# SyncE reads the first role straight from the input; the first chunks of W_down and x change queues

## The chip, the cores and the metric

One core of one Trainium2 chip. The metric is device time in microseconds of one launch. The core has TensorE (PE, with PEld for its weight loads), VectorE (DVE), ScalarE (ACT), GpSimd (POOL) and SyncE (SP), and 16 DMA engines that all queues share. A name with q behind it (SPq, ACTq) is the engine's sequencer, where register loads and the issuing of DMAs show.

## What is computed

For each of 8 batches an adapter is chosen by a role number (0 to 2). With `x` of 512 rows by 1024:

```python
h = einsum('bsh,bhk->bsk', x, W_down[role]) + b_down[role]   # K = 512
h = gelu(h)
u = einsum('bsk,bkh->bsh', h, W_up[role]) + b_up[role]
y = x + u
out = layernorm(y) * gamma[role] + beta[role]
```

All is f32. The eight role numbers are the input `roles`.

## The kernel before

Every operand of a matmul is held as two parts, hi (the value rounded to fp32r by ScalarE) and lo (the rest, subtracted by VectorE), and each product is made of three passes, hi by hi, hi by lo, lo by hi. A batch has a down stage (96 matmuls of 128x512, line 254) and an up stage (96 matmuls, line 261), so TensorE runs 16 stages of 96 matmuls.

`x` (transposed, `xT`) and `W_down` come in four parts (`NLOAD`) of 128x1024, each made of two chunks of 512 columns. ScalarE casts a part (`x_hi`, L331; `wd_hi`, L335), VectorE subtracts (`x_lo`, L498; `wd_lo`, L503), TensorE multiplies. Part 0 of batch 0 alone is loaded, and cast, as two separate chunks: x at L219 and L220, W_down at L223 and L224, cast at L445, L447, L449 and L451. ScalarE casts these in a fixed order: x chunk 0, x chunk 1, W_down chunk 0, W_down chunk 1. TensorE starts the first down stage when x chunk 0 and W_down chunk 0 are cast (L283, L284); its second group of 24 matmuls needs part 1 of both.

W_down is picked by the role of the batch, so its address needs the role in a register of SyncE. ScalarE's first instruction is the DMA of the eight roles into the tile `roles_sb` (L440), the second that of `b_down` (L441); SyncE issues both x chunks, waits for `roles_landed` (L221), reads the role with `load_role` (a register load from the tile, a range check by register operations and an assertion, L140), and then issues W_down's chunks and, alternating, the other parts of x and W_down and the four parts of W_up (L161, L164, L174), all on its own queue. Then come, in a hand-written order with semaphore waits, the loads for batch 1, `b_up`, the rows of x, gamma and beta.

While data is on the way TensorE runs `WARM_UP` = 12 matmuls of bf16 zeros (L320, L321), from the moment VectorE has cleared their tile (L641). ScalarE's wait for GpSimd's constants and a first Gelu that loads the activation table (L443) stand between its DMA issues and its first cast.

Behind the up stage, per 128-row tile, VectorE adds bias rows (`bias_tile`, L520) and the residual (`sum_tile`, L525), ScalarE makes mean and variance (L369 to L372), GpSimd the inverse deviation (L467, L469), VectorE centres and finishes (L542, L556), and a DMA stores. VectorE's work is in one hand-written order, in which the `h_lo` parts (L513) that the next up stage waits for (L315) stand behind bias tiles and the splits for the next batch.

Of the kernel before, what the change touches and what calls it, by code (L numbers as in the profile page):

```python
# [16 lines left out]
def bass_role_adapter_layernorm(  # L17
# [11 lines left out]
):  # L29
    B, S, H = x.shape  # L30
    R, _, K = W_down.shape
    HC = H // P
    KC = K // P
    NT = S // P
    NLOAD = 4
    CPL = HC // NLOAD
    BANK = 512
    HALVES = H // BANK
    WARM_UP = 12
    assert KC == NLOAD and S == BANK and K == BANK and HALVES == 2 and NT == 4 and CPL == 2  # L40

    with ExitStack() as ctx:  # L42
        def sb(name, shape, dt):
            return ctx.enter_context(nc.sbuf_tensor(name, shape, dt))

        def sem(name):
            return ctx.enter_context(nc.semaphore(name))


        x_stage = sb("x_stage", [P, NLOAD, CPL * S], F32)  # L50
        wd_stage = sb("wd_stage", [P, NLOAD, CPL * K], F32)
# [39 lines left out]
        roles_landed = sem("roles_landed")  # L91
# [6 lines left out]
        first_x_landed = sem("first_x_landed")  # L98
        first_wd_landed = sem("first_wd_landed")
# [36 lines left out]
        scaled = sem("scaled")  # L136
        normed = sem("normed")

        def load_role(eng, batch):
            return eng.value_load(roles_sb[0:1, bass.ds(batch, 1)], min_val=0, max_val=R - 1)  # L140

# [2 lines left out]
        def is_first(batch):  # L144
            return isinstance(batch, int) and batch == 0

        def is_last(batch):
            return isinstance(batch, int) and batch == B - 1
# [2 lines left out]

        @block.sync
        def _(sp):
            def x_src(batch):
                return xT[batch].rearrange("(p n c) s -> p n (c s)", n=NLOAD, c=CPL)

            def wd_src(role):
                return W_down[role].rearrange("(p n c) k -> p n (c k)", n=NLOAD, c=CPL)

            def load_x_part(batch, i):  # L160
                sp.dma_start(x_stage[:, i, :], x_src(batch)[:, i, :]).then_inc(x_landed[i], 16)  # L161

            def load_wd_part(role, i):
                sp.dma_start(wd_stage[:, i, :], wd_src(role)[:, i, :]).then_inc(wd_landed[i], 16)  # L164

            def load_ahead(batch, role, i):

                sp.wait_ge(x_split, NLOAD * (batch - 1) + i + 1)
                load_x_part(batch, i)
                sp.wait_ge(wd_split, NLOAD * (batch - 1) + i + 1)  # L170
                load_wd_part(role, i)

            def load_wu_part(role, i):
                sp.dma_start(wu_stage[:, i, :], W_up[role, i * P:(i + 1) * P, :]).then_inc(wu_landed[i], 16)  # L174

            def load_rows(b, t):
                if not is_first(b):
                    sp.wait_ge(stored[t], 16 * b)
                sp.dma_start(rows[:, t, :], x[b, t * P:(t + 1) * P, :]).then_inc(rows_landed[t], 16)

            def load_role_row(row, param, role, landed):
                sp.dma_start(row[:, :], param[bass.ds(role, 1), :].partition_broadcast(P)).then_inc(landed, 16)

            def store_last(t):
                b = B - 1
                sp.wait_ge(normed, NT * b + t + 1)
                sp.dma_start(out[b, t * P:(t + 1) * P, :], rows[:, t, :]).then_inc(stored[t], 16)

            def steps(b):
                first, last = is_first(b), is_last(b)  # L190
                role = load_role(sp, b)
                load_rows(b, 0)
                load_rows(b, 1)
                if not first:
                    load_rows(b, 2)
                    sp.wait_ge(normed, NT * b)
                load_role_row(gamma_row, gamma, role, gamma_landed)
                load_role_row(beta_row, beta, role, beta_landed)
                if first:
                    load_rows(b, 2)  # L200
                load_rows(b, 3)
                if last:
                    return
                next_role = load_role(sp, b + 1)
                if first:
                    for i in range(1, NLOAD):
                        load_ahead(1, next_role, i)
                for i in range(KC):
                    sp.wait_ge(wu_split, KC * b + i + 1)
                    load_wu_part(next_role, i)  # L210
                sp.wait_ge(biased, NT * (b + 1))
                load_role_row(b_up_row, b_up, next_role, b_up_landed)
                if isinstance(b, int) and b + 2 == B:
                    return
                role_after = load_role(sp, b + 2)
                for i in range(NLOAD):
                    load_ahead(b + 2, role_after, i)

            sp.dma_start(x_stage[:, 0, 0:S], x_src(0)[:, 0, 0:S]).then_inc(first_x_landed, 16)  # L219
            sp.dma_start(x_stage[:, 0, S:CPL * S], x_src(0)[:, 0, S:CPL * S]).then_inc(x_landed[0], 16)  # L220
            sp.wait_ge(roles_landed, 16)  # L221
            first_role = load_role(sp, 0)
            sp.dma_start(wd_stage[:, 0, 0:K], wd_src(first_role)[:, 0, 0:K]).then_inc(first_wd_landed, 16)  # L223
            sp.dma_start(wd_stage[:, 0, K:CPL * K], wd_src(first_role)[:, 0, K:CPL * K]).then_inc(wd_landed[0], 16)  # L224
            for i in range(1, NLOAD):
                load_x_part(0, i)
                load_wd_part(first_role, i)
            for i in range(KC):
                load_wu_part(first_role, i)
            load_ahead(1, load_role(sp, 1), 0)  # L230
            load_role_row(b_up_row, b_up, first_role, b_up_landed)
            steps(0)
            with sp.Fori(1, B - 2) as b:
                steps(b)
            steps(B - 2)
            steps(B - 1)
            for t in range(NT - 1):
                store_last(t)
            for i in range(HALVES):
                sp.wait_ge(normed, NT * B + i)  # L240
                half = slice(i * BANK, (i + 1) * BANK)
                sp.dma_start(out[B - 1, (NT - 1) * P:NT * P, half], rows[:, NT - 1, half]).then_inc(last_stored, 16)
            for t in range(NT - 1):
                sp.wait_ge(stored[t], 16 * B)
            sp.wait_ge(stored[NT - 1], 16 * (B - 1))
            sp.wait_ge(last_stored, 16 * HALVES)

        @block.tensor
        def _(pe):
# [69 lines left out]
            pe.wait_ge(zeros_ready, 1)  # L319
            for _ in range(WARM_UP):  # L320
                pe.matmul(up_ps[:, 0, 0:BANK], squares[:, 0:P], squares[:, 0:BANK], start=True, stop=True)  # L321
# [6 lines left out]
        def _(act):  # L328
# [24 lines left out]
            def store(b, t):  # L353
                act.wait_ge(normed, NT * b + t + 1)
                act.dma_start(out[b, t * P:(t + 1) * P, :], rows[:, t, :]).then_inc(stored[t], 16)
# [54 lines left out]
            def steps(b):  # L410
# [26 lines left out]
                if not last:  # L437
                    store(b, 1)

            act.dma_start(roles_sb[:, :], roles).then_inc(roles_landed, 16)  # L440
            act.dma_start(b_down_all[:, :], b_down_cols).then_inc(b_down_landed, 16)  # L441
            act.wait_ge(constants_ready, 2)
# [236 lines left out]
```

## Time and profile before

| what | us |
|---|---|
| three timed runs | 366.93, 367.15, 368.8 |
| median of them | 367.15 |
| the profiled execution | 365.34 |
| span of its instructions | 363.5 |
| TensorE busy | 353.5 (97% of the span) |
| VectorE, ScalarE, GpSimd busy | 287.7, 185.9, 40.4 |
| the chain that ended last, by engine | PE 96%, DMA 1% |

The span runs from the first to the last instruction; the execution's own time is 1.84 us longer (365.34 to 363.5). The chain that ended last names at each step what released the next; share of it on an engine is time that only this engine's work could shorten.

### The profile page before, as it was taken

To read this page: it belongs to the slowest core of one execution; us is meant where nothing else is said; L and a number is where in the kernel's file an instruction comes from. 1 tells how busy PE (TensorE), PEld (TensorE's weight loads), DVE (VectorE), ACT (ScalarE), POOL (GpSimd) and SP (SyncE) were. 2 spreads that over 40 slices of the span, in tenths; PEclk is the share of its full clock that TensorE was granted. 3 is DMA by queue.
4 is the path that set the end of the run, shared out by engine and by line. 5 is a ranking of instruction groups with operands and counts; after the bars stand their busy time and mean duration, and the time that the engine had idled before them with its cause. 6 is when DMAs were issued, how large, how long until landed. Compare 5 with 4: busy or idle time off the path is not lost.

```text
span 363.5 us, 4942 instructions
## 1 busy us (share of the span) xinstructions
PE 353.5 (97%) x1548; PEld 289.8 (80%) x1548; DVE 287.7 (79%) x293; ACT 185.9 (51%) x297; POOL 40.4 (11%) x71
## 2 busy tenths in 40 slices
PE   7999999999999999999999999999999999999991
PEld 3888888888888888888888888888888888888880
DVE  2897989897896889968798687977789777864474
ACT  4893556671646536563385733656255561714132
POOL 0000221002200212002110021100310012200011
PEclk9999999999999999999999999999999999999998
DMA  7999999979868977869787896778977812580023
GB/s 210 408 404 412 409 404 401 330 272 377 304 231 288 308 293 261 272 252 331 248 264 247 284 374 222 224 273 276 392 267 231 289 58 101 200 278 0 0 115 116
DMA packets 27083, 96.59 MB, mean 266 GB/s; under 512 B 3138, under 2 KB 3138, under 8 KB 27074
## 3 DMA queue, kind: packets, MB, share of 16 engines
q1 hardware_dynamic: 22896, 81.80, 63.2%
q10 hardware_dynamic: 4178, 14.69, 10.5%
q8 instruction: 4, 0.07, 0.1%
q14 instruction: 5, 0.04, 0.1%
HBM read 79.70 MB, written 16.78 MB: 265 GB/s over the span
## 4 chain that ended last, share of the span: by engine, by line
PE 96%; DMA 1%; ACT 0%; DVE 0%; POOL 0%; issue 0%; SPq 0%; DVEq 0%; POOLq 0%; ACTq 0%
PE down_ps L254 48%; PE up_ps L261 48%; DMA wd_stage<-W_down 1%; DMA roles_sb<-roles 0%; DVE rows L556 0%; POOL half_var L475 0%; DVE rows L533 0%; SPq L140 0%; DVEq L42 0%; ACT wd_hi L449 0%; ACT squares L389 0%; POOLq L42 0%; ACT neg_mean_scaled L382 0%; POOL var_eps L478 0%; ACT neg_mean L384 0%
## 5 line engine op out<-in xcount | busy, mean ns | idle before, releaser
L254 PE MATMUL down_ps<-x_hi,wd_hi 128*128 128x512 f32 x256 | 81.5, 389 | 1.0 <-ACT wd_hi L449 1.0
L254 PE MATMUL down_ps<-x_lo,wd_hi 128*128 128x512 f32 x256 | 81.4, 389 | 0.0
L254 PE MATMUL down_ps<-x_hi,wd_lo 128*128 128x512 f32 x256 | 81.4, 389 | 0.0
L261 PE MATMUL up_ps<-wu_hi,h_hi 128*128 128x512 f32 x256 | 79.6, 389 | 0.0
L261 PE MATMUL up_ps<-wu_lo,h_hi 128*128 128x512 f32 x256 | 79.5, 389 | 0.0
L261 PE MATMUL up_ps<-wu_hi,h_lo 128*128 128x512 f32 x256 | 79.4, 389 | 0.0
L254 PEld LDWEIGHTS down_ps<-x_hi,wd_hi 128*128 128x128 f32 x256 | 48.0, 188 | 11.5 <-issue 1.5
L261 PEld LDWEIGHTS up_ps<-wu_hi,h_hi 128*128 128x128 f32 x256 | 48.0, 188 | 10.2 <-issue 0.3
L261 PEld LDWEIGHTS up_ps<-wu_lo,h_hi 128*128 128x128 f32 x256 | 48.0, 188 | 10.0
L254 PEld LDWEIGHTS down_ps<-x_hi,wd_lo 128*128 128x128 f32 x256 | 48.0, 188 | 10.0
L254 PEld LDWEIGHTS down_ps<-x_lo,wd_hi 128*128 128x128 f32 x256 | 48.0, 188 | 10.0
L261 PEld LDWEIGHTS up_ps<-wu_hi,h_lo 128*128 128x128 f32 x256 | 48.0, 188 | 9.9
L556 DVE SCALAR_TENSOR_TENSOR rows<-h_full,rstd,beta_row 128x1024 f32<-128x1024 f32 (+1 forms) x33 | 41.2, 1250 | 18.3 <-POOL rstd L469 17.0
L369 ACT ACTIVATE neg_mean_scaled<-row_sum 128x1 f32<-128x1 f32 x31 | 6.3, 203 | 85.7 <-DVE rows L525 85.7
L467 POOL TENSOR_TENSOR var_eps<-var,eps 128x1 f32<-128x1 f32 x31 | 15.4, 498 | 312.1 <-ACT squares L372 312.1
L542 DVE SCALAR_TENSOR_TENSOR h_full<-rows,neg_mean,gamma_row 128x1024 f32<-128x1024 f32 (+1 forms) x33 | 41.2, 1250 | 6.1 <-ACT neg_mean L370 5.5
L498 DVE TENSOR_TENSOR x_lo<-x_stage,x_hi 128x1024 fp32r<-128x1024 f32 x32 | 39.1, 1221 | 7.4 <-ACT x_hi L447 4.0
L331 ACT CAST x_hi<-x_stage 128x1024 fp32r<-128x1024 f32 x31 | 32.6, 1051 | 23.2 <-PE down_ps L254 10.4
L513 DVE TENSOR_TENSOR h_lo<-h_full,h_hi 128x512 fp32r<-128x512 f32 x32 | 22.1, 691 | 28.2 <-ACT h_hi L364 28.2
L525 DVE SCALAR_TENSOR_TENSOR rows<-up_ps,rows 128x1024 f32<-128x1024 f32 x31 | 37.8, 1220 | 7.7 <-PE up_ps L261 7.7
L362 ACT ACTIVATE h_full<-down_ps,b_down_all 128x512 f32<-128x512 f32 x32 | 22.0, 688 | 41.5 <-PE down_ps L254 41.5
L503 DVE TENSOR_TENSOR wd_lo<-wd_stage,wd_hi 128x1024 fp32r<-128x1024 f32 x32 | 39.0, 1218 | 1.6 <-ACT wd_hi L451 1.3
(37 smaller groups left out, 250.9 us busy)
## 6 DMA issues: line engine op xcount, KB each, us to landing
wu_stage<-W_up SPq DMA_DIRECT2D x32, 512.0 KB, 6.9
rows<-x SPq DMA_DIRECT2D x32, 512.0 KB, 3.5
x_stage<-xT SPq DMA_DIRECT2D x31, 512.0 KB, 8.5
wd_stage<-W_down SPq DMA_DIRECT2D x31, 512.0 KB, 8.8
out<-rows ACTq DMA_DIRECT2D x28, 512.0 KB, 4.6
b_up_row<-b_up SPq DMA_DIRECT2D x8, 512.0 KB, 3.8
gamma_row<-gamma SPq DMA_DIRECT2D x8, 512.0 KB, 6.3
beta_row<-beta SPq DMA_DIRECT2D x8, 512.0 KB, 7.1
```

The lines of the kernel that those rows point to most:

```text
L254: return pe.matmul(down_ps[:, kc, :], wd_part[:, n, c * K + kc * P:c * K + (kc + 1) * P], x_part[:, n, c * S:(c + 1) * S], start=start, st ...
L261: mm = pe.matmul(up_ps[:, t % 2, half], h_part[:, kc, t * P:(t + 1) * P], wu_part[:, kc, half], start=(kc == 0 and h_part is h_hi and wu_p ...
L331: act.copy(x_hi[:, i, :], x_stage[:, i, :]).then_inc(x_hi_ready, 1)
L362: act.activation(h_full[:, kc, :], down_ps[:, kc, :], ACT.Gelu, bias=bias).then_inc(h_full_ready, 1)
L369: act.mul(neg_mean_scaled[:, t:t + 1], row_sum[:, t:t + 1], -1.0 / H * H ** -0.5).then_inc(scaled_mean_ready, 1)
L467: pool.tensor_tensor(var_eps[:, t:t + 1], var[:, t:t + 1], eps[:, :], ALU.add).then_inc(var_eps_ready, 1)
L498: dve.tensor_tensor(x_lo[:, i, :], x_stage[:, i, :], x_hi[:, i, :].bitcast(F32), ALU.subtract).then_inc(x_split, 1)
L503: dve.tensor_tensor(wd_lo[:, i, :], wd_stage[:, i, :], wd_hi[:, i, :].bitcast(F32), ALU.subtract).then_inc(wd_split, 1)
L513: dve.tensor_tensor(h_lo[:, kc, :], h_full[:, kc, :], h_hi[:, kc, :].bitcast(F32), ALU.subtract).then_inc(h_split, 1)
L525: dve.scalar_tensor_tensor(out=rows[:, t, :], in0=up_ps[:, t % 2, :], scalar=1.0, in1=rows[:, t, :], op0=ALU.mult, op1=ALU.add, accum_out= ...
L542: dve.scalar_tensor_tensor(out=centred[:, t % 2, half], in0=rows[:, t, half], scalar=neg_mean[:, t:t + 1], in1=gamma_row[:, half], op0=ALU ...
L556: dve.scalar_tensor_tensor(out=rows[:, t, half], in0=centred[:, t % 2, half], scalar=rstd[:, t:t + 1], in1=beta_row[:, half], op0=ALU.mult ...
```

## The change

SyncE no longer waits for the roles at the start. It loads the first role into a register directly from the input in HBM, issues W_down's chunk 0, x's chunk 1 and W_down's chunk 1, and goes on as before; its wait for `roles_landed` moves to the first later use of the tile. x's chunk 0 becomes ScalarE's first DMA, ahead of the roles and b_down. The warm-up has 9 matmuls in place of 12.

```diff
-    WARM_UP = 12
+    WARM_UP = 9
...
+        def x_src(batch):
+            return xT[batch].rearrange("(p n c) s -> p n (c s)", n=NLOAD, c=CPL)
+
...
-            sp.dma_start(x_stage[:, 0, 0:S], x_src(0)[:, 0, 0:S]).then_inc(first_x_landed, 16)
+
+            first_role = sp.value_load(roles[0:1, 0:1], min_val=0, max_val=R - 1)
+            sp.dma_start(wd_stage[:, 0, 0:K], wd_src(first_role)[:, 0, 0:K]).then_inc(first_wd_landed, 16)
             sp.dma_start(x_stage[:, 0, S:CPL * S], x_src(0)[:, 0, S:CPL * S]).then_inc(x_landed[0], 16)
-            sp.wait_ge(roles_landed, 16)
-            first_role = load_role(sp, 0)
-            sp.dma_start(wd_stage[:, 0, 0:K], wd_src(first_role)[:, 0, 0:K]).then_inc(first_wd_landed, 16)
             sp.dma_start(wd_stage[:, 0, K:CPL * K], wd_src(first_role)[:, 0, K:CPL * K]).then_inc(wd_landed[0], 16)
             for i in range(1, NLOAD):
                 load_x_part(0, i)
                 load_wd_part(first_role, i)
             for i in range(KC):
                 load_wu_part(first_role, i)
+            sp.wait_ge(roles_landed, 16)
             load_ahead(1, load_role(sp, 1), 0)
...
+            act.dma_start(x_stage[:, 0, 0:S], x_src(0)[:, 0, 0:S]).then_inc(first_x_landed, 16)
             act.dma_start(roles_sb[:, :], roles).then_inc(roles_landed, 16)
             act.dma_start(b_down_all[:, :], b_down_cols).then_inc(b_down_landed, 16)
```

## Rows read from the trace of the kernel before

**Rows 1.** The page: busy time, share of the span, instructions.

```profile
PE 353.5 (97%) x1548; PEld 289.8 (80%) x1548; DVE 287.7 (79%) x293; ACT 185.9 (51%) x297; POOL 40.4 (11%) x71
```

**Rows 2.** The chain that ended last, in time order: start us, duration us, what.

```profile
0.73 1.18 DMA roles_sb<-roles
1.92 0.46 SPq L140
...
2.88 3.46 DMA wd_stage<-W_down
...
6.36 0.63 ACT wd_hi L449
...
7.12 22.04 PE down_ps L254 x96
...
72.69 21.89 PE up_ps L261 x96
```

**Rows 3.** Timeline of 0 to 14 us: start, duration, engine, line, operation, idle before.

```profile
0.73 0.39 SPq L219 DMA_DIRECT2D x_stage<-xT  x1
0.73 0.53 ACTq L440 DMA_DIRECT2D roles_sb<-roles  x1
...
1.18 0.42 SPq L220 DMA_DIRECT2D x_stage<-xT  x1
1.18 4.97 PE L321 MATMUL up_ps<-squares 128*128 128x512 bf16 x12 [1.18 <-DVE squares L641]
...
1.70 1.28 ACT L443 ACT_TABLE_LOAD   x1 [1.57 <-PEq L672]
...
3.41 0.34 SPq L224 DMA_DIRECT2D wd_stage<-W_down  x1
3.57 0.62 ACT L445 CAST x_hi<-x_stage 128x512 fp32r<-128x512 f32 x1 [0.38 <-DMA x_stage<-xT]
...
4.46 0.62 ACT L447 CAST x_hi<-x_stage 128x512 fp32r<-128x512 f32 x1 [0.26 <-DMA x_stage<-xT]
...
7.01 0.62 ACT L451 CAST wd_hi<-wd_stage 128x512 fp32r<-128x512 f32 x1
...
10.62 1.05 ACT L335 CAST wd_hi<-wd_stage 128x1024 fp32r<-128x1024 f32 x1 [0.30 <-DMA wd_stage<-W_down]
...
12.69 1.52 PE L254 MATMUL down_ps<-x_hi,wd_hi 128*128 128x512 f32 x6
```

**Rows 4.** Line 140, all engines: duration ns min/median/max, first and last start.

```profile
L140 SPq TENSOR_LOAD <-roles_sb x23: 263/269/463, 1.9 to 291.6; - x23
```

**Rows 5.** Timeline of the warm-up: two successive weight loads.

```profile
4.99 0.15 PEld L321 LDWEIGHTS up_ps<-squares 128*128 128x128 bf16 x1 [0.28 <-issue]
...
5.42 0.15 PEld L321 LDWEIGHTS up_ps<-squares 128*128 128x128 bf16 x1 [0.27 <-issue]
```

**Rows 6.** Stretches: busy time per engine, granted clock, DMA share, GB/s.

```profile
2.00:3.00 1.00, 1.00 (x4) 0.45 (x3) 0.00 (x0) 0.99 (x2) 0.00 (x0) 1.00 0.90 244
...
4.00:5.00 1.00, 1.00 (x4) 0.31 (x3) 0.00 (x0) 0.74 (x2) 0.00 (x0) 1.00 0.75 209
```

**Rows 7.** Timeline of ACT, 34 to 78 us.

```profile
36.06 1.06 ACT L335 CAST wd_hi<-wd_stage 128x1024 fp32r<-128x1024 f32 x1 [0.18 <-DMA wd_stage<-W_down]
37.09 0.20 ACT L369 ACTIVATE neg_mean_scaled<-row_sum 128x1 f32<-128x1 f32 x1
```

**Rows 8.** Timeline of DVE, 34 to 78 us.

```profile
67.18 1.22 DVE L520 TENSOR_TENSOR rows<-rows,b_up_row 128x1024 f32<-128x1024 f32 x1 [1.43 <-DMA rows<-x]
...
75.80 0.69 DVE L513 TENSOR_TENSOR h_lo<-h_full,h_hi 128x512 fp32r<-128x512 f32 x1
```

**Rows 9.** Timeline of PE, 34 to 78 us.

```profile
76.15 0.61 PE L261 MATMUL up_ps<-wu_hi,h_lo 128*128 128x512 f32 x2
76.64 0.70 PE L261 MATMUL up_ps<-wu_hi,h_hi 128*128 128x512 f32 x2
```

More of the change, by code:

```diff
@@ L153, in _ @@
         def _(sp):
-            def x_src(batch):
-                return xT[batch].rearrange("(p n c) s -> p n (c s)", n=NLOAD, c=CPL)
             def wd_src(role):
```

## Prediction

> **What bounds the kernel now.** I read the page first: TensorE is busy 97% of the span [rows 1]. So only three things can move the time: when the first real matmul starts, holes between the 16 stages, and what follows the last matmul. The chain in order of time says how the start comes about [rows 2]: the DMA of the roles takes 1.18 us from its issue at 0.73, SyncE's register load 0.46 more, W_down's chunk 0 is issued at 2.88 and takes 3.46 us to land, its cast takes 0.63, and TensorE begins at 7.12. From there the stages follow each other in 21.76 us, which is 0.2267 us for each of 96 matmuls, two rows shown excepted: 22.04 for the first, 21.89 for the up stage of batch 1. The change touches only what lies ahead of 7.12, and the supply of data behind it. The timeline shows the start's other actors [rows 3]: x's two chunks are cast at 3.57 and 4.46, long before W_down's chunk 0 is there.
>
> **SyncE's role.** Removed from the path are the wait for the roles' DMA and the load from the tile; added is one register load from HBM, which starts where SyncE issued its first DMA, at 0.73. No row shows such a load. Its floor is the fastest load from the tile, 0.263 us [rows 4]. Its ceiling is a whole DMA fetch of the same bytes and then the slowest load from the tile on SyncE, 1.18 + 0.463 = 1.64 us [rows 2, 4]. It is one instruction without descriptors, a write or a semaphore, so it lies nearer to the row of its own kind: I take 0.72, a third of the way up. Behind the load came register operations, the range check and the assertion, from 1.92 + 0.46 = 2.38 to the issue at 2.88, that is 0.50 us; they stay. So W_down's chunk 0 is issued at 0.73 + 0.72 + 0.50 = 1.95, with ends 1.49 and 2.87: 0.93 earlier, between 1.39 and 0.01. The Trainium skill (Runtime: NRT & Kernel Launch, the section on the preamble and postamble) puts a register load from HBM in the preamble at about 1.3 us, for several registers. By that page's figure, as an estimate, the issue would be at 2.53, 0.35 earlier; no row here shows it.
>
> **x's chunks.** Chunk 0 goes out at 0.73 again, from ScalarE's queue, and landed in 2.84 us before (cast at 3.57, right behind its landing) [rows 3]. ScalarE's own order gets one more DMA issue ahead of the table load, 0.53 us at most by the row of its first issue. The table load then ends at 1.70 + 0.53 + 1.28 = 3.51, the small Gelu (0.2 us) at some 3.75, and the cast of x chunk 0 at about 4.4. That is hidden: nothing needs it before chunk 0 of W_down is cast. The roles and b_down are issued 0.53 later, and their first readers come well behind 10 us (SyncE's load for batch 1, ScalarE's first bias); hidden as well.
>
> Chunk 1 of x is what counts. It was issued at 1.18 and cast at 4.46 [rows 3]. Now it stands behind W_down's chunk 0 on SyncE: one issue spacing later (2.88 to 3.41, 0.53 us, less a register operation; I take 0.50), so at 2.45. ScalarE's order is unchanged: it casts x chunk 1 **before** W_down chunk 0. The start therefore hangs on x chunk 1's landing and then on two casts. Its time to land has three rows: 2.84 us (x chunk 0, nothing ahead), 4.46 - 1.18 = 3.28 (x chunk 1, one chunk ahead), 7.01 - 3.41 = 3.60 at most (W_down chunk 1, one ahead) [rows 3]. I take 3.1, since the DMA engines are not full all the time there (0.90 and 0.75 busy in two of these microseconds [rows 6]) and the queue is emptier: landed and picked up at 5.55. Then one cast spacing of 0.65 (6.36 to 7.01 [rows 2, 3]) and the 0.76 from the cast of W_down's chunk 0 to the first matmul (6.36 to 7.12 [rows 2]): TensorE starts at 6.96, **0.16 us earlier** of the 0.93 that the earlier issue promised. Ends: 1.49 + 0.50 + 2.84 + 1.41 = 6.24, 0.9 earlier; and 2.87 + 0.50 + 3.60 + 1.41 = 8.38, 1.3 later. W_down's chunk 1 is issued some 0.5 behind x chunk 1 and cast in turn; TensorE has four matmuls of cover for it, 0.9 us.
>
> **The next data.** Part 1 of W_down is cast by 10.62 + 1.05 = 11.67, and TensorE comes to it at 12.69 [rows 3]: 1.0 us of slack, so a start up to 1.0 us earlier finds it ready. Its DMA is not issued later than before unless the register load is at its ceiling.
>
> Further on an earlier start is less free. In the up stage of batch 1, VectorE's last `h_lo` ends at 75.80 + 0.69 = 76.49 [rows 8], and TensorE starts the group that needs it at 76.64, 0.49 behind the last pair's start where 0.453 is the rule, with a first pair of 0.70 us where 0.61 is [rows 9]: this is the wait in the 21.89. So VectorE is already 0.13 us late there. What fixes VectorE's time? It waited 1.43 us for a DMA of x's rows at 67.18 [rows 8], and before that ScalarE's first mean came at 37.09, directly behind a cast that had waited for W_down's DMA (36.06 + 1.06 = 37.12) [rows 7]. These transfers stand in a queue that has been full since the start; they move only as far as the start of the queue fills better, which I put between 0 and 0.3 us, nearest to 0.1. Whatever TensorE gains above that at the start, it can lose again at 76.6. A loss at the start is never given back, TensorE having no holes to close but this 0.13.
>
> **Warm-up.** Three fewer matmuls at 0.427 us (weight loads at 4.99 and 5.42 [rows 5]) end the warm-up at about 1.18 + 9 * 0.427 = 5.02 in place of 6.15. They cost nothing themselves. But by their spacing they ran at 1.2 GHz (512 columns in 0.427 us), though the granted clock in the stretches reads 1.00 there [rows 6]; the real ones at 0.227 us run at 2.4 GHz; the twelve fill 4.97 us in all [rows 3], less than 12 * 0.427 = 5.12 in spite of a drain at the end, so the clock rose within the last two of them, behind the place where nine would end. If it doesn't rise in the same way, real matmuls run at 0.427 in place of 0.227, 0.2 us lost on each. The floor is 0; as a ceiling, if ten of them ran so, as the first ten of the warm-up did, 2.0 us. In the forecast I take 0: 9 of the 10 that preceded the rise are still there, and real work follows. The Trainium skill (TensorE: Matmul & The Clock Gate, part 1) says that the number of slow matmuls differs from run to run of one kernel. No row of one profile can show that; if it holds, the fewer warm-ups cost something in some runs only.
>
> **The sum.** Start -0.16, given back at batch 1 down to about -0.1, warm-up 0, end untouched: -0.1 us. Against the profiled execution that is 365.34 - 0.1 = 365.2 (span 363.4). The profiled execution lies 1.8 us below the median of the runs, 367.15; carried over, the forecast is 367.0.
>
> **The rivals.** (a) The start gains fully: the load is at its floor and the first matmul starts near 6.2, and VectorE's chain follows since DMAs move too: -0.9, 366.3. For it: 0.75 busy in the microsecond from 4 us [rows 6], so transfers can pack closer. Against it: the lateness at 76.5. (b) **Slower: x chunk 1 lands late.** The register load from HBM takes over about 0.9 us, and ScalarE, waiting for x chunk 1, holds the finished W_down chunk back. Break-even: 7.12 - 1.41 - 3.1 - 0.50 - 0.50 - 0.73 = 0.88 us of load; at 1.64 us and the longest landing it costs 1.3: 368.4; at 1.3 us it would be +0.4. For it: even a DMA of 32 bytes, the roles', took 1.18 us [rows 2]. (c) Slower by the clock: five of the real matmuls slow, +1.0, up to 2.0: 368.1. For it, the rise lay behind the ninth. (d) Nothing happens because the roles weren't the limit: with the chunk order swapped, the three first chunks land no sooner than the DMA engines deliver them; 367.15.
>
> **How the numbers follow.** Forecast (start between 6.7 and 7.2, with (d) inside it) 0.50; (a) 0.15; (b) 0.15; (c) 0.20. A measurement of this kernel tells a change from none at about 0.5%, 1.8 us; the three runs themselves lie 1.9 us apart. No case of faster reaches it alone, -0.9 being its end: 0.04, for scatter of the runs. (b) with (c) together reach 3.3 and either with scatter could: 0.06. Same: 0.90. The range goes from (a), 366.3, less part of that scatter to 365.7, and up to the ends of (b) and (c), 368.5.
>
> **What would show it.** The first `wd_hi` cast directly behind that of x chunk 1, with no DMA wait between: right; a wait there means W_down still limits. The register load of SyncE on the input at 0.5 to 0.9 us. First matmul of line 254 at 6.7 to 7.2 us. First down stage 22.0 us; 23 or more means a slow clock. Up stage of batch 1 longer than 21.89 by about what the start gained. A first matmul before 6.2 or after 8.4, or a time outside the range, would prove the sum wrong.

## The result, and the profile after

The changed kernel takes 367.88 us (median of 22 runs, 367.34 to 369.02); the kernel before, run beside it, 366.51 us (22 runs, 365.69 to 369.62). The ratio is 1.0032, with a 95% interval of 1.0018 to 1.0047: **slower by 0.3%**. The forecast was a hair faster. The profiled execution took 367.57 us, with a span of 365.7 where it was 363.5.

The page of the changed kernel, busy time first, then the page's slices of the granted clock:

```profile
PE 354.1 (97%) x1545; PEld 290.5 (79%) x1545; DVE 287.7 (79%) x293; ACT 185.7 (51%) x297; POOL 40.5 (11%) x71
...
PEclk9899999999999999999999999999999999999996
```

TensorE does the same real work [rows 1], and it is busy 0.6 us more: slower matmuls, less three warm-ups. The slices are 9.1 us each, and the second isn't at full clock. The chain of the changed kernel in order of time (start us, duration us, what):

```profile
0.71 0.86 SPq L220
...
1.60 0.69 SPq L220
...
2.79 0.40 SPq L221
...
3.24 3.25 DMA x_stage<-xT
...
6.51 0.62 ACT x_hi L448
7.12 0.53 ACT wd_hi L450
...
7.79 23.65 PE down_ps L254 x96
31.44 21.76 PE up_ps L261 x96
...
74.96 21.83 PE up_ps L261 x96
```

Read it against [rows 2]. The roles' DMA is gone from the chain, and W_down's is too: what TensorE now waits for, through ScalarE's fixed order of casts, is **x's chunk 1**, issued at 3.24 where it used to go out at 1.18. The first matmul starts at 7.79 in place of 7.12, 0.67 us later. The first down stage takes 23.65 in place of 22.04, 1.61 more. The up stage of batch 1 takes 0.06 less. 0.67 + 1.61 - 0.06 = 2.2 us, the whole difference of the spans. (The medians differ by 1.4 us. Each profile is a single execution, and the timed runs of the changed kernel lie up to 1.7 us apart, those of the kernel before 3.9.)

The source view of the line that loads the role (duration ns, min/median/max; start) shows what one `value_load` from HBM is:

```profile
L220 SPq TENSOR_LOAD <-roles_ptr x1: 859/859/859, 0.7 to 0.7; - x1
L220 SPq TENSOR_LOAD <-roles x1: 694/694/694, 1.6 to 1.6; - x1
```

Two loads one after the other: first the tensor's address (`roles_ptr`), then the value, together 1.58 us from 0.71 to 2.29 with the gap [compare rows 4, one load of 0.263 to 0.463 us from the tile]. W_down's chunk 0 goes out at 2.79 in place of 2.88: of the 0.93 us that the forecast had for this issue, 0.09 is left. The timeline of the changed kernel:

```profile
0.73 0.39 ACTq L440 DMA_DIRECT2D x_stage<-xT  x1
...
1.18 3.99 PE L321 MATMUL up_ps<-squares 128*128 128x512 bf16 x9 [1.18 <-DVE squares L642]
...
3.24 0.43 SPq L222 DMA_DIRECT2D x_stage<-xT  x1
...
3.57 0.62 ACT L446 CAST x_hi<-x_stage 128x512 fp32r<-128x512 f32 x1
...
6.51 0.62 ACT L448 CAST x_hi<-x_stage 128x512 fp32r<-128x512 f32 x1 [2.32 <-DMA x_stage<-xT]
7.03 0.61 ACT L450 CAST wd_hi<-wd_stage 128x512 fp32r<-128x512 f32 x1
...
7.55 0.62 ACT L452 CAST wd_hi<-wd_stage 128x512 fp32r<-128x512 f32 x1
...
7.79 3.21 PE L254 MATMUL down_ps<-x_hi,wd_hi 128*128 128x512 f32 x8 [2.62 <-ACT wd_hi L450]
...
12.75 1.06 ACT L335 CAST wd_hi<-wd_stage 128x1024 fp32r<-128x1024 f32 x1 [0.24 <-DMA wd_stage<-W_down]
```

ScalarE waited 2.32 us for x's chunk 1 (the row at 6.51). Before the cast of W_down's chunk 0 at 7.03 (L450) stands no wait at all: that chunk was there already. The first eight real matmuls take 3.21 us, 0.40 each where 0.227 is the rule. Why is in the stretches (busy time per engine, then granted clock, DMA share, GB/s). First one row of the kernel before, then the changed kernel:

```profile
3.00:4.00 1.00, 1.00 (x4) 0.31 (x3) 0.00 (x0) 0.62 (x2) 0.00 (x0) 1.00 0.85 246
```

```profile
3.00:4.00 1.00, 1.00 (x4) 0.31 (x3) 0.00 (x0) 0.99 (x3) 0.00 (x0) 1.00 0.17 42
4.00:5.00 1.00, 1.00 (x3) 0.15 (x1) 0.00 (x0) 0.18 (x1) 0.00 (x0) 1.00 0.80 252
...
7.00:8.00 1.00, 0.21 (x1) 0.24 (x2) 0.84 (x1) 1.00 (x3) 0.00 (x0) 1.00 0.89 111
8.00:9.00 1.00, 1.00 (x4) 0.81 (x4) 1.00 (x2) 0.17 (x1) 0.00 (x0) 0.71 0.60 188
9.00:10.00 1.00, 1.00 (x4) 0.71 (x3) 0.52 (x1) 0.00 (x0) 0.00 (x0) 0.50 0.82 291
10.00:11.00 1.00, 1.00 (x4) 0.81 (x3) 0.00 (x0) 0.00 (x0) 0.00 (x0) 0.50 1.02 389
11.00:12.00 1.00, 1.00 (x4) 0.77 (x4) 0.00 (x0) 0.54 (x1) 0.00 (x0) 0.59 1.03 422
```

Two things are to be seen. **The clock**: TensorE does nothing from 5.17 to 7.79, 2.62 us, and the granted clock then falls, 0.71 from 8 to 9 us and 0.50 for the next two: seven real matmuls with records of over 0.6 us where 0.39 is usual. It was high at the start, for the first three real matmuls start at 7.79, 8.10 and 8.33, close together; it fell behind them. **The DMA engines**: from 3 to 4 us they are 0.17 busy, where the kernel before had 0.85 in that microsecond, and 0.90 and 0.75 in those beside it [rows 6]. x's chunk 0 is through, and SyncE has issued nothing before 2.79. The data behind come later too: part 1 of W_down is cast at 12.75 in place of 10.62 [rows 3]. Not all of these 2.1 us can be put down to the hole. Four profiles of this document have none in this microsecond (0.68 to 0.85 busy: the kernel before with 12, 16, 14 and 9 warm-ups), and that cast starts at 10.62, 11.37, 11.91 and 12.15 in them; in the eight that have one there (0.07 to 0.21 busy) it starts at 12.31 to 13.62. A hole goes with later data, but the 10.62 of the first profile is the earliest of them all.

### The profile page after: what moved, and what is told of

Same layout as the page of the kernel before. It is cut to its first block, busy times and chain, and to the rows that moved or that the text cites. A ratio compares the mean times of both kernels' runs of the same rounds, so it can differ in the third digit from the quotient of the medians.

```text
span 365.7 us, 4937 instructions
## 1 busy us (share of the span) xinstructions
PE 354.1 (97%) x1545; PEld 290.5 (79%) x1545; DVE 287.7 (79%) x293; ACT 185.7 (51%) x297; POOL 40.5 (11%) x71
## 3 DMA queue, kind: packets, MB, share of 16 engines
q10 hardware_dynamic: 4322, 14.95, 10.6%
## 4 chain that ended last, share of the span: by engine, by line
PE 96%; DMA 1%; ACT 1%; SPq 1%; DVE 0%; POOL 0%; issue 0%; DVEq 0%; POOLq 0%; ACTq 0%
PE down_ps L254 48%; PE up_ps L261 48%; DMA x_stage<-xT 1%; SPq L220 0%; DVE rows L557 0%; POOL half_var L476 0%; DVE rows L534 0%; DVEq L42 0%; ACT x_hi L448 0%; ACT squares L389 0%; POOLq L42 0%; ACT wd_hi L450 0%; SPq L221 0%; ACT neg_mean_scaled L382 0%; POOL var_eps L479 0%
## 5 line engine op out<-in xcount | busy, mean ns | idle before, releaser
L254 PE MATMUL down_ps<-x_hi,wd_hi 128*128 128x512 f32 x256 | 82.6, 395 | 2.6 <-ACT wd_hi L450 2.6
L254 PEld LDWEIGHTS down_ps<-x_hi,wd_hi 128*128 128x128 f32 x256 | 48.6, 190 | 13.6 <-issue 3.5
L509 DVE TENSOR_TENSOR wu_lo<-wu_stage,wu_hi 128x1024 fp32r<-128x1024 f32 x32 | 38.6, 1222 | 1.3 <-ACT wu_hi L351 1.1
```

The costliest lines, as they stand in the source:

```text
L254: return pe.matmul(down_ps[:, kc, :], wd_part[:, n, c * K + kc * P:c * K + (kc + 1) * P], x_part[:, n, c * S:(c + 1) * S], start=start, st ...
L509: dve.tensor_tensor(wu_lo[:, i, :], wu_stage[:, i, :], wu_hi[:, i, :].bitcast(F32), ALU.subtract).then_inc(wu_split, 1)
```

## The experiments

All times "before" are of the kernel before, run beside on the same chip.

**More warm-ups in the changed kernel.**

```diff
-    WARM_UP = 9
+    WARM_UP = 12
```

> The changed kernel with the warm-up of before (12 in place of 9). Theory (the loss has two parts: the first real matmul starts 0.67 us later, and TensorE's longer idle time of 2.6 us ahead of it lets the clock fall, worth the 1.6 us by which the first down stage grew): the start stays at 7.8 us, the idle time shrinks to 1.6 us, the first down stage is 22.0 to 22.2 us in the profile, and the time is about 1 us below the changed kernel's, 366.8 to 367.2 where before is 366.5. Rival (the slow matmuls are chance, whatever the warm-up; only the late start counts): first stage now long, now short, and a median like the changed kernel's, 1.3 us above before.

Measured: 367.55 us (before 366.33), ratio 1.0012, interval 0.9987 to 1.0037. In the profile TensorE starts at 8.17 and the first stage is again 23.65 us:

```profile
8.17 3.27 PE L254 MATMUL down_ps<-x_hi,wd_hi 128*128 128x512 f32 x8 [2.20 <-ACT wd_hi L450]
```

The idle time ahead of it is 2.20 us, and the clock fell as before, with seven matmuls of over 0.6 us. The start was later than in the changed kernel because the same register load took 0.86 + 1.03 us this time, so that 2.2 us were still idle and the theory's 22.0 us for the stage isn't tested by this profile.

The timed runs say more than the profile. Each lists its mean granted clock over the whole span. In the fourteen profiles of this document that mean is 0.984 to 0.992 in the seven that have slow real matmuls and 0.992 to 0.996 in the seven that have none. With 12 warm-ups, seven of 12 runs list 0.994 or more, and three of these took 366.06 to 366.60 us; of the 34 runs of the changed kernel with nine, one lists 0.994, none more, and none is under 367.22 us. So 12 warm-ups seem to spare many runs the fall; the profiled one, at 0.987 and 367.91 us, wasn't among them.

**Fewer warm-ups in the kernel before.**

```diff
-    WARM_UP = 12
+    WARM_UP = 9
```

> The kernel before with 9 warm-up matmuls, nothing else. Theory: the start stays at 7.12, TensorE idles 2.0 us ahead of it in place of 1.0, the clock falls or rises late in part of the runs, and the median is 0.5 to 1.0 us above before. Rival (clock by chance, whatever the warm-up): same as before within 0.2 us, so that all of the change's 1.3 us would have to come from the start and the order of the transfers.

Measured: 367.24 us (before 366.33), ratio 1.0016, interval 0.9992 to 1.0041: not resolved. The median is 0.9 us up, as the theory had it, and the interval holds the rival too. The profile is of one of the faster runs (366.38). W_down's chunk came 0.3 us earlier in this execution and TensorE started at 6.80, after 1.72 us of idle time; the clock didn't fall:

```profile
13.34 16.58 PE down_ps L254 x72
29.93 21.76 PE up_ps L261 x96
...
73.45 4.10 PE up_ps L261 x18
77.55 0.09 issue
77.63 17.96 PE up_ps L261 x78
```

Before 13.34 the chain runs over other engines, because TensorE waited there (0.83 us) for part 1 of W_down, cast at 12.15 in this execution with no hole in the DMA engines' work. The chain also shows a hole of 0.09 us at 77.55, the place that the forecast named from [rows 8, 9] (the stage lasts 22.14 in all). A start 0.3 us earlier ended the first down stage at 29.93, 0.76 us later than in the profile of before. So this profile shows a cost of late data and none of the clock. Four of the 12 timed runs list a mean granted clock of 0.988, lower than in any profile without slow matmuls, against six of 35 at 0.989 or less for the kernel before: whether nine warm-ups cost something by themselves stays open.

**The casts in the order of arrival.**

```diff
-            act.wait_ge(x_landed[0], 16)
-            act.copy(x_hi[:, 0, S:CPL * S], ...).then_inc(x_hi_ready, 1)
             act.wait_ge(first_wd_landed, 16)
             act.copy(wd_hi[:, 0, 0:K], wd_stage[:, 0, 0:K]).then_inc(first_wd_hi, 1)
+            act.wait_ge(x_landed[0], 16)
+            act.copy(x_hi[:, 0, S:CPL * S], ...).then_inc(x_hi_ready, 1)
```

> The changed kernel, but ScalarE casts W_down's chunk 0 before x's chunk 1. Theory (x's chunk 1, landing at 6.49, holds the start): W_down's chunk 0, issued at 2.79, lands at 5.7 to 6.2, TensorE starts at 6.4 to 6.9, some 1 us earlier than 7.79, and its second four matmuls may wait a little for chunk 1; the time falls by 0.7 to 1.5 us against the changed kernel. Rival (the three chunks come off the DMA engines nearly together, so the order of casts is worth one cast only): start at 7.2 to 7.3, time 0.5 us lower.

Measured: 367.54 us (before 366.33), ratio 1.0024, interval 1.0003 to 1.0045. The start moved as expected, to 6.77:

```profile
6.01 0.62 ACT L448 CAST wd_hi<-wd_stage 128x512 fp32r<-128x512 f32 x1 [1.72 <-DMA wd_stage<-W_down]
...
6.77 3.45 PE L254 MATMUL down_ps<-x_hi,wd_hi 128*128 128x512 f32 x8 [2.08 <-ACT wd_hi L448]
```

and nothing came of it. The chain reaches the up stage in the same place as the changed kernel's 31.44:

```profile
14.81 16.60 PE down_ps L254 x72
31.42 21.76 PE up_ps L261 x96
```

TensorE did its first 24 matmuls, seven of them slow after 2.08 us of idle time, and then waited for W_down's part 1 until 14.81. So x's chunk 1 holds the **start**, as the theory had it, but in this execution, with part 1 cast at 13.62, a start a microsecond earlier was worth nothing. In the medians the version lies 1.2 us above the kernel before, where the changed kernel lies 1.4: the 0.7 us and more that the theory had didn't come.

**x's chunk 1 on ScalarE's queue.**

```diff
-            sp.dma_start(x_stage[:, 0, S:CPL * S], x_src(0)[:, 0, S:CPL * S]).then_inc(x_landed[0], 16)
...
             act.dma_start(x_stage[:, 0, 0:S], x_src(0)[:, 0, 0:S]).then_inc(first_x_landed, 16)
+            act.dma_start(x_stage[:, 0, S:CPL * S], x_src(0)[:, 0, S:CPL * S]).then_inc(x_landed[0], 16)
             act.dma_start(roles_sb[:, :], roles).then_inc(roles_landed, 16)
```

> The changed kernel with x's chunk 1 as ScalarE's second DMA, behind chunk 0, in place of SyncE's queue behind W_down's chunk 0; 9 warm-ups. Theory: chunk 1 lands by 4.6, the DMA engines are no longer idle from 3 to 4 us, W_down's chunk 0 (issued at 2.79 still) lands at 5.9 to 6.3 and TensorE starts at 6.6 to 7.1, as before or slightly earlier; the time falls 0.7 us or more against the changed kernel, and what then remains against before (0 to 0.6) is the clock. Rival (the register load from HBM is the whole loss): no change of the start, 7.7 or later.

Measured: 367.93 us (before 366.33), ratio 1.002, interval 0.9995 to 1.0045. The profile has the rival's number, a start at 7.84, by a load that took longer still. Its source view:

```profile
L220 SPq TENSOR_LOAD <-roles_ptr x1: 1472/1472/1472, 0.7 to 0.7; - x1
L220 SPq TENSOR_LOAD <-roles x1: 1321/1321/1321, 2.2 to 2.2; - x1
```

2.79 us in place of 1.55, beside the transfers of both x chunks. W_down's chunk goes out at 4.03, and the DMA engines are 0.02 busy from 4 to 5 us. TensorE idles 2.65 us, and again 0.64 us behind its first four matmuls, and the clock falls for 14 matmuls. This execution, at 369.70 us, is the slowest of the 12. Five of the others took 366.07 to 366.87 us, less than any run of the changed kernel, so in part of the runs the theory's gain seems to have come; no trace shows one of these.

**The order of the transfers alone, in the kernel before.** The role still comes through the tile.

```diff
-            sp.dma_start(x_stage[:, 0, S:CPL * S], x_src(0)[:, 0, S:CPL * S]).then_inc(x_landed[0], 16)
             sp.wait_ge(roles_landed, 16)
             first_role = load_role(sp, 0)
             sp.dma_start(wd_stage[:, 0, 0:K], wd_src(first_role)[:, 0, 0:K]).then_inc(first_wd_landed, 16)
+            sp.dma_start(x_stage[:, 0, S:CPL * S], x_src(0)[:, 0, S:CPL * S]).then_inc(x_landed[0], 16)
```

> The kernel before, role still by the tile and 12 warm-ups; only x's chunk 1 is issued behind W_down's chunk 0, the casts in their old order. Theory (the order of the transfers costs by itself): chunk 1 goes out at about 3.3, lands at 6.4 to 6.7, TensorE starts at 7.8 to 8.1, the DMA engines stand nearly idle between 3 and 4 us; time 0.7 to 1.2 us above before. Rival (the register load from HBM is what costs): start at 7.1 to 7.3, as before.

Measured: 368.08 us (before 366.27), ratio 1.0052, interval 1.0034 to 1.0070. Its chain, and the stretch in which the DMA engines run dry:

```profile
3.39 3.19 DMA x_stage<-xT
...
6.61 0.62 ACT x_hi L447
7.22 0.53 ACT wd_hi L449
...
7.89 23.60 PE down_ps L254 x96
31.49 21.76 PE up_ps L261 x96
```

```profile
3.00:4.00 1.00, 1.00 (x4) 0.31 (x3) 0.00 (x0) 0.41 (x2) 0.00 (x0) 1.00 0.11 24
```

This is the changed kernel's picture, line for line (7.89, 23.60, 31.49 against 7.79, 23.65, 31.44; 0.11 against 0.17 busy), without any load from HBM and with twelve warm-ups. **The place of x's chunk 1 is enough to bring about the whole loss.** The time rests on four executions, 367.51 to 368.58 us.

**The load from HBM alone, in the kernel before.**

```diff
             sp.dma_start(x_stage[:, 0, S:CPL * S], x_src(0)[:, 0, S:CPL * S]).then_inc(x_landed[0], 16)
-            sp.wait_ge(roles_landed, 16)
-            first_role = load_role(sp, 0)
+            first_role = sp.value_load(roles[0:1, 0:1], min_val=0, max_val=R - 1)
```

> The kernel before with the source of the role alone changed: both x chunks go out first on SyncE, then it loads the role from HBM, without waiting for the roles' DMA; 12 warm-ups. Theory (a load from HBM is two loads, of the tensor's address and of the value, 0.86 + 0.69 us on idle DMA engines and 1.3 to 1.5 us each beside x's transfers, as in the run with x's chunk 1 on ScalarE's queue): the load lasts from 1.6 to 4.2 to 4.6, W_down's chunk 0 goes out at 4.6 to 5.0, TensorE starts at 8.5 to 9.2; time 1.5 to 2.5 us above before. Rival (those 2.8 us were chance): load 1.6 us, W_down out at 3.7, start at 7.8 to 8.0.

Measured: 368.21 us (before 366.27), ratio 1.0045, interval 1.0030 to 1.0061. The chain:

```profile
1.64 1.65 SPq L221
...
3.32 0.50 SPq L221
...
4.32 3.23 DMA wd_stage<-W_down
...
8.33 24.84 PE down_ps L254 x96
```

The load costs 2.15 us in all, between theory and rival, most of it in the address. This execution is the slowest of five (369.21 us). W_down goes out at 4.32, 1.44 us later than through the tile, whose DMA had been on its way since 0.73 while SyncE issued x. TensorE starts at 8.33.

**Order of arrival throughout, in the kernel before**: the order of the transfers as in the run with the order alone, and the casts as in the run with the casts swapped.

> The kernel before with x's chunk 1 issued behind W_down's chunk 0 and ScalarE's casts in the order of arrival: x 0, W_down 0, x 1, W_down 1; role by the tile, 12 warm-ups. Theory: W_down's chunk 0, issued at 2.88 with only x's chunk 0 ahead of it, lands after 2.8 to 3.0 us in place of 3.46; TensorE starts at 6.4 to 6.7 in place of 7.12, may wait up to 0.6 us for chunk 1 four matmuls later, and the time is 0.2 to 0.5 us below before at best. Rival (an earlier start is lost again in the first down stage, whose part 1 comes when the DMA engines bring it, and in the up stage of batch 1, where VectorE is late already): first stage and up stage of batch 1 grow by as much as the start gains, time the same as before.

Measured: 367.75 us (before 366.27), ratio 1.0034, interval 1.0021 to 1.0047. The start is the earliest of all, 6.62, and the kernel is slower:

```profile
6.62 1.17 PE L254 MATMUL down_ps<-x_hi,wd_hi 128*128 128x512 f32 x4 [1.16 <-ACT wd_hi L447]
...
8.05 1.17 PE L254 MATMUL down_ps<-x_hi,wd_hi 128*128 128x512 f32 x4 [0.27 <-ACT wd_hi L451]
...
12.54 1.05 ACT L335 CAST wd_hi<-wd_stage 128x1024 fp32r<-128x1024 f32 x1 [0.23 <-DMA wd_stage<-W_down]
...
13.73 1.61 PE L254 MATMUL down_ps<-x_hi,wd_hi 128*128 128x512 f32 x6 [0.88 <-ACT wd_hi L335]
```

The rival was right. Four matmuls, then a hole until 8.05 for W_down's chunk 1; after 20 more, a wait of 0.88 us until 13.73 for part 1 of W_down. The first matmul of the up stage starts at 30.46 where it was 29.00, and the two up stages behind it have holes as well (22.2 and 22.7 us long). No matmul was slow in this execution, the slowest of six (368.06 us; the fastest took 367.09): its loss is data alone.

**Eighteen warm-ups in the changed kernel**, so that TensorE has no idle time ahead of the start.

```diff
-    WARM_UP = 9
+    WARM_UP = 18
```

> The changed kernel with 18 warm-ups, which fill TensorE's idle time up to about 7.1 us when the clock rises near 5.1. Theory (the idle time ahead of the start, 2.6 us with 9 and 2.2 with 12, makes the clock fall): no slow real matmul, first down stage 22.0 to 22.2 us, start 7.8 to 8.2, time 1 to 1.5 us below the changed kernel: 366.4 to 366.9. Rival (the slow matmuls come by chance whatever TensorE does before): 7 or more slow real matmuls again, 367.5 to 368.

Measured: 366.97 us (before 366.27), ratio 1.0021, interval 1.0010 to 1.0031. Chain and stretches:

```profile
8.13 22.15 PE down_ps L254 x96
30.28 21.76 PE up_ps L261 x96
```

```profile
8.00:10.00 2.00, 1.87 (x8) 1.46 (x9) 1.73 (x2) 0.62 (x1) 0.00 (x0) 1.00 0.84 268
```

The start is later than in the changed kernel, 8.13, and the up stage begins 1.16 us earlier, at 30.28: no slow matmul, 1.00 granted throughout.

**More warm-ups in the kernel before**: `WARM_UP = 16`, and 14.

> The kernel before with 16 warm-ups, so that TensorE is busy up to 7.0 us when the clock rises near 5.5. Theory (idle time ahead of the start and a late rise cost part of the runs up to 2 us, and before with 12 warm-ups has 1.0 us of idle time): the runs of 367 and more become rarer, the median falls by 0 to 0.4 us to 366.0 to 366.4, the start stays at 6.9 to 7.3. Rival (the scatter of before comes from when the data arrive, not from the clock): the same median and scatter; and where the clock rises late, the warm-up itself reaches past 7.1 and delays the start, up to 0.5 us slower.

> The kernel before with 14 warm-ups, which end at 6.4 to 6.8. Theory: between before and the run with 16, median 366.1 to 366.4 and the same start. Rival (12 is already enough and what is left is the arrival of data): same as before within 0.1 us.

Measured: 366.64 us with 16 (before 366.55), ratio 1.0003, interval 0.9987 to 1.0019; 366.39 us with 14, ratio 0.9997, interval 0.9977 to 1.0017. Neither differs from before. Their profiles also show how much W_down's first chunk scatters: it was cast at 6.83 and 7.27 where [rows 2] has 6.36, with the same issue time to 0.02 us.

**The changed kernel and its version with 18, side by side.**

> The changed kernel as it is, once more, beside its version with 18 warm-ups on the same chip. Theory (both terms, late start and slow clock): 1.1 to 1.6 us above before, 6 or more slow real matmuls in the profile. Rival (the first profile's slow matmuls were bad luck): fewer than 3 slow matmuls, and a time like that of the version with 18.

> The changed kernel with 18 warm-ups, once more. Theory: no slow real matmul, 0.5 to 0.9 us above before and 0.5 to 1 us below the changed kernel of the same call: the late start alone. Rival (filling the idle time changes nothing but the chip did): the same time as the changed kernel.

Measured, beside before at 366.45: 367.62 us with nine (ratio 1.0029, interval 1.0007 to 1.0052) and 367.09 us with 18 (ratio 1.0030, interval 1.0011 to 1.0048). The medians differ by 0.5 us as expected, the ratios don't: this pair alone doesn't decide. Over both sets of runs, none of 34 with nine warm-ups is under 367.22 us, and 16 of 23 with 18 are; and 20 of the 34 list a mean granted clock of 0.991 or less, where one of the 23 does. The profile with nine has six slow matmuls after 3.27 us of idle time, the one with 18 none.

**All profiles in one view.** Idle time of TensorE between warm-up and first real matmul, and matmuls with records of over 0.6 us:

| kernel | starts at | idle ahead | slow matmuls |
|---|---|---|---|
| before | 7.12 | 0.98 | 0 |
| before, 9 warm-ups | 6.80 | 1.72 | 0 |
| before, order of arrival | 6.62 | 1.16 | 0 |
| before, 14 | 8.03 | 0.75 | 0 |
| before, 16 | 7.60 | none | 0 |
| changed, 18 (two profiles) | 8.13, 7.83 | 0.16, none | 0, 0 |
| changed, casts swapped | 6.77 | 2.08 | 7 |
| before, x chunk 1 late | 7.89 | 2.19 | 7 |
| changed, 12 | 8.17 | 2.20 | 7 |
| changed (two profiles) | 7.79, 7.93 | 2.62, 3.27 | 7, 6 |
| changed, x chunk 1 on ScalarE | 7.84 | 2.65 | 14 |
| before, load from HBM | 8.33 | 2.97 | 13 |

Every profile with 2.08 us or more of idle time shows the granted clock at 0.50 afterwards, and none with 1.72 or less does, whatever the number of warm-ups. That is what TensorE did before the clock fell, in fourteen executions; that idle time alone decides isn't shown.

The timed runs set two limits to this reading. Of the 100 timed runs of the kernel before in these sets, 14 list a mean granted clock of 0.991 or less and took 367.02 to 369.12 us: its clock seems to fall too, in some executions, whose idle times aren't known. And ten of the 34 runs with nine warm-ups list 0.993 and took 368.10 to 368.76 us, about a microsecond more than the two profiled ones (0.987 at 367.57 us, 0.991 at 367.39). None of the ten has a trace, and what makes them long stays open. A clock that hadn't risen yet at the first real matmul, as rival (c) had it, isn't excluded, for the granted clock reads 1.00 even while warm-ups run 0.427 us apart.

## Why the prediction was wrong

Two terms of the sum failed. The register load was taken as 0.72 us and measured 1.58, which made the start 0.67 us later where -0.16 was forecast; and the slow clock was put at nothing, where the first down stage of the profile grew by 1.61 us, all of it in its first 24 matmuls.

**What bounds the kernel** held: nothing behind the first down stage changed but 0.06 us, and the end not at all.

**SyncE's role: the term that was mis-sized.** Taken as 0.72 us, with ends 0.26 and 1.64; from 0.71 to 2.29 it measured 1.58, almost the ceiling. The forecast counted one load of the kind in [rows 4]; an HBM tensor takes two, the address first. The break-even that the prediction gave, 0.88 us, was thus passed by 0.7. The Trainium skill's figure (Runtime: NRT & Kernel Launch, the section on the preamble and postamble) of about 1.3 us for the preamble's register loads from HBM was nearer than the value taken from the tile's rows. The trace has 1.58 us for the pair; single loads here ran from 0.50 to 1.65 us.

**x's chunks** held as a mechanism: ScalarE did wait for chunk 1 with W_down's chunk at hand. With the measured load the prediction's own sum gives 0.71 + 1.58 + 0.50 + 0.45 + 3.27 + 0.52 + 0.76 = 7.79, the start that was measured. The 3.1 us taken for the landing was near, with 3.27 measured from issue to cast, and the two casts stood 0.52 us apart and not 0.65. Chunk 0 was cast from 3.57 to 4.19 where the prediction had about 4.4, which mattered as little as it said.

**The next data: a limit that was missed.** The prediction said that the DMA of W_down's part 1 is not issued later than before unless the load is at its ceiling, and left it there. The load was near its ceiling, with x's chunk 1 now ahead in the same queue, and that DMA went out at 4.85 in place of 4.41. More than this delay counted, as far as the runs show, that for a microsecond the 16 DMA engines had almost nothing to do. Moving x's chunk 1, which needs no role, behind the wait for the role took away the work that filled that wait. In the changed kernel's own profile TensorE waits for no data behind its first matmul, since the slow clock brings it to part 1 later still; but in the runs with the casts swapped, with the order of arrival and, once, with 18 warm-ups (a wait of 0.31 us until 13.98) part 1 is what TensorE waits for, and an earlier start is lost there. That an earlier start is lost again further on was foreseen for the up stage of batch 1, where it is small. The 1.0 us of slack that the prediction gave part 1 was luck of its one profile: with nine warm-ups in the kernel before, TensorE waited 0.83 us for it without any hole.

**Warm-up: 0 was taken, and the reason given fell short.** The prediction looked at when the clock rises. It had risen ahead of the first real matmul in all five profiles with nine warm-ups; in one of them it had fallen again by then. What the prediction didn't look at is that a later start and an earlier end of the warm-up make an idle time, 0.98 us before and 2.62 after. That term measures some 1 us in the profiles (the up stage begins at 31.4 and 31.3 us with nine, 30.3 and 30.6 with 18) and 0.5 us in the medians of the pair run side by side, whose ratios don't show it. Late start and fewer warm-ups both have a part: the profile with 12 still had 2.20 us of idle time, by the late start, while the timed runs with 12 list the lower clock less often. The Trainium skill (TensorE: Matmul & The Clock Gate, part 1) was cited for a number of slow matmuls that differs from run to run of one kernel. The traces agree: of the changed kernel's two profiles, one has all nine warm-ups 0.427 us apart, the other is faster behind its seventh, and the real matmuls hold 7 and 6 slow ones.

**The numbers.** Rivals (b) and (c) came true together, though in the profiles the slow clock followed the idle time and not a late rise. With 18 warm-ups the medians lie 0.7 and 0.6 us above the kernel before; by that, as an estimate, about 0.7 of the 1.4 us is the late start with its later data and the rest the clock. That the range still holds 367.88 is luck: the forecast's base was 0.6 us too high, since the median of the first three runs, 367.15, became 366.51 with 22, and 1.4 us on top of 367.15 would have lain at its upper end, 368.5. The case "same within 0.5%", at 0.90, is where the result lies.

**Left open.** How the loss divides in the timed runs is known only roughly, since the load (1.55 to 1.89 us beside one x chunk), W_down's landing (over 1.2 us) and the clock all scatter, and the long runs at a mean clock of 0.993 have no trace. Among the eleven other kernels none is shown to beat the one before.

## What to carry to other kernels

Before a transfer that must wait for a value, issue whatever needs no value: a queue that waits while the DMA engines run dry makes the data behind it late, and in the two kernels here that started earlier all the same (6.77 and 6.62) nothing was won. Price a register load from an HBM tensor as two dependent loads on the sequencer, against a DMA that runs while the same sequencer issues other work. And when a start moves, look at TensorE's idle time ahead of it: cover it with warm-up up to the start that is measured, not the one that is hoped for. One profile gives neither the slack of a transfer nor the place where the clock rises: both moved by more than a microsecond between executions.

## What the runs showed of the hardware

- A `value_load` from a tensor in HBM is two loads: 0.84 to 0.92 us and then 0.69 to 1.03 us in six profiles with one x chunk in flight, 1.47 + 1.32 and 1.65 + 0.50 us with two. From a tile in SBUF it is one, 0.46 us the first time.
- Idle times of TensorE of 2.08 to 3.27 us ahead of the first real matmul were each followed by a granted clock of 0.50 and 6 to 14 matmuls at 0.427 us spacing; idle times up to 1.72 us by none.
- The warm-ups, 0.427 us apart at first, became faster behind the seventh (at 3.7 us) in two profiles and behind the 15th (at 7.1 us) in two.
- A microsecond in which the 16 DMA engines were 0.07 to 0.21 busy, in eight profiles, went with W_down's part 1 ready at 12.3 to 13.6 us; in four with 0.68 to 0.85 busy it was ready at 10.6 to 12.2.
- The same 256 KB transfer, issued at 2.88 to 2.90 in four profiles of kernels that are alike up to there, was ready to cast 3.14, 3.48, 3.94 and 4.37 us later.
